# Attention B of a three-stage kernel: five batches in flight, memory summed in PSUM, norms on another engine, a new value operand, one bank of scores

## What is computed

```python
SEG, N_HEADS, dk = 64, 16, 8
def step(carry, qkv):                       # 4 segments of 64 rows, one after the other
    M, z = carry
    q, k, v = qkv
    sq = _sigma(q)                          # elu(x) + 1 = max(x, 0) + exp(min(x, 0))
    denom_q = jnp.sum(sq * z[:, :, None, :], axis=-1, keepdims=True) + EPS
    A_mem = jnp.matmul(sq, M) / denom_q
    scores = jnp.matmul(q, jnp.swapaxes(k, -2, -1)) * inv_sqrt_dk
    scores = jnp.where(causal, -jnp.inf, scores)
    A_dot = jnp.matmul(jax.nn.softmax(scores, axis=-1), v)
    A_s = beta * A_mem + (1.0 - beta) * A_dot
    sk = _sigma(k)
    denom_k = jnp.sum(sk * z[:, :, None, :], axis=-1, keepdims=True) + EPS
    V_prev = jnp.matmul(sk, M) / denom_k
    M_new = M + jnp.einsum('bhtk,bhtv->bhkv', sk, v - V_prev)
    z_new = z + jnp.sum(sk, axis=-2)
    return ((M_new, z_new), A_s)
```

## Time and profile before

| | us |
|---|---|
| median of 3 runs | 1576.78 |
| lowest and highest | 1570.99, 1587.72 |
| the profiled execution | 1586.89 |
| its span, first to last instruction | 1585.1 |
| of it, attention B | from 959.5 to the end |

### The profile page before, as it was taken

How to read it: one execution, slowest core, us unless ns; L and a number is a source line. 1 busy time by engine, 2 the same in 40 slices (tenths; PEclk the granted TensorE clock), 3 DMA queues, 4 the chain that set the end, 5 groups by cost and what they waited for, 6 DMA issues and landing times. The chain is left out here.

```text
span 1585.1 us, 52984 instructions
## 1 busy us (share of the span) xinstructions
PE 1328.7 (84%) x16996; PEld 1165.0 (73%) x16996; DVE 1095.4 (69%) x3074; ACT 873.5 (55%) x2020; POOL 927.5 (59%) x1340
## 2 busy tenths in 40 slices
PE   5999999999999999999477873787887778887786
PEld 4898998899888988999456652576666667666675
DVE  4467787788777887888344444667677777767874
ACT  2466766666666666676356652444454544444442
POOL 4456766667667666775478873445445554444551
PEclk9899999999999999999789995879799998879996
DMA  4523322332233223331144422434344444334331
GB/s 136 159 85 104 101 77 82 89 99 80 79 89 99 78 81 89 99 91 51 44 127 121 134 70 74 111 109 119 105 127 119 116 121 124 106 104 117 112 117 46
DMA packets 181701, 158.23 MB, mean 100 GB/s; under 512 B 12529, under 2 KB 163185, under 8 KB 181618
## 3 DMA queue, kind: packets, MB, share of 16 engines
q1 hardware_dynamic: 181618, 157.17, 35.1%
HBM read 113.09 MB, written 44.04 MB: 99 GB/s over the span
## 5 line engine op out<-in xcount | busy, mean ns | idle before, releaser
L609 PE MATMUL a_bank<-a_vp,a_prob 128*128 128x74 f32 x4096 | 598.0, 253 | 0.0
L609 PEld LDWEIGHTS a_bank<-a_vp,a_prob 128*128 128x128 f32 x4096 | 587.8, 192 | 5.5
L697 DVE TENSOR_REDUCE a_nmax<-a_bank 128x2 f32<-128x512 f32 x512 | 344.9, 685 | 156.9 <-PE a_bank L578 156.7
L496 ACT ACTIVATE a_prob<-a_bank 128x512 f32<-128x512 f32 x512 | 305.5, 597 | 216.0 <-PE a_bank L593 210.7
L578 PE MATMUL a_bank<-a_k_st,a_q_st 96*128 96x256 bf16 x1024 | 259.5, 276 | 38.3 <-DVE a_nmax L697 25.2
L593 PE MATMUL a_bank<-a_q_st,a_k_st 120*128 120x256 bf16 x1024 | 281.5, 275 | 2.2 <-POOL a_q_st L345 2.2
L416 POOL TENSOR_TENSOR a_prod<-a_ov,a_wgt 128x512 f32<-128x512 f32 x128 | 152.5, 1192 | 34.1 <-POOL a_prod L416 17.2
L345 POOL TENSOR_SCALAR a_q_st<-a_mt 24x2048 bf16<-24x2048 bf16 x64 | 121.5, 1898 | 82.6 <-ACT a_mt L470 36.9
L578 PEld LDWEIGHTS a_bank<-a_k_st,a_q_st 96*128 96x128 bf16 x1024 | 128.9, 134 | 50.0 <-DVE a_nmax L697 32.1
L1504 ACT ACTIVATE c_prob<-c_bank 128x256 f32<-128x256 f32 x256 | 98.8, 386 | 101.4 <-PE c_bank L1596 97.1
L593 PEld LDWEIGHTS a_bank<-a_q_st,a_k_st 120*128 120x128 bf16 x1024 | 140.1, 137 | 11.0 <-issue 2.6
(11 more groups left out here) (205 smaller groups left out, 2821.2 us busy)
## 6 DMA issues: line engine op xcount, KB each, us to landing
a_q_st<-scratch_a_parts_dram SPq DMA_DIRECT2D x64, 288.0 KB
a_k_st<-scratch_a_parts_dram SPq DMA_DIRECT2D x192, 96.0 KB
c_q_st<-scratch_c_parts_dram SPq DMA_DIRECT2D x64, 288.0 KB
c_k_st<-scratch_c_parts_dram SPq DMA_DIRECT2D x192, 96.0 KB
scratch_a_parts_dram<-a_parts SPq DMA_DIRECT2D x32, 384.0 KB, 2.7
scratch_c_parts_dram<-c_parts SPq DMA_DIRECT2D x32, 384.0 KB, 2.7
a_x<-in_x SPq DMA_DIRECT2D x32, 128.0 KB, 3.5
scratch_y<-a_y SPq DMA_DIRECT2D x32, 128.0 KB, 3.1
```

Of the source, the lines that this page charges most:

```text
L496: act.activation(prob[h % 4][:, :, :].rearrange("p a b -> p (a b)"), t_ps[h % 2][:, :], ACT.Exp).then_inc(exped, 1)
L609: mm = pe.matmul(o_ps[g % 2][:, at:at + VM], prob[h % 4][:, c, t * P:(t + 1) * P], vp[o][:, c, 0:VM], start=c == 0, stop=c == NT - 1)
L697: dve.tensor_reduce(nmax[:, t, 2 * g:2 * g + 2, 0], s_ps[t][:, :].rearrange("p (h k) -> p h k", h=2), AX.X, ALU.max, negate=True).then_inc ...
```

## The change

- Five batches are in flight in place of four. Of the memory, segment 0 stays at lag 1 (steps 6 and 7) and segments 1 and 2 move to the next iteration, lag 2 (steps 1, 2 and 4, 5). x4's chain moves to lag 4.
- The memory is summed in PSUM: update 1 and 2 add to what is in ps_c. DVE masks the sum once a segment, and the addition to mz and the tile mzt are gone. Reads go to other columns of the same bank.
- z4 is normalised on ACT and not on DVE. POOL computes the statistics of both norms in one set of four instructions at the start of its body, ahead of the split.
- max(kq, 0) is made by ACT (Relu), min(kq, 0) by POOL after the split, both by DVE before. The factor 8^-0.5 moves from q into the exponential's scale.
- The value operand vb is copied by ACT straight from PSUM in two instructions; the tile vs and POOL's four copies are gone.
- There is one bank of scores in place of two. Score units are at steps 1, 3, 5, 7. The maxima are split once a batch, 32 wide. The freed bank lets z and z4 have their own (ps_d).
- The shifted units start at step 3 of lag 2 (OFF = 3) and end at step 2 of lag 3. Before they started at step 7 of lag 1.
- SP issues half 0 of batch n at the end of its body as before, but half 1 of batch n - 1 near the start of the next body.
- The transposes of z, z4, ad and am are written as matmuls against the identity in two column halves. Those of sg and of the maxima stay transposes.
- The kq matmuls move from step 1 to step 0, and z's transpose from step 0 to step 7 of the iteration before.

```diff
-        S_AT = (1, 2, 4, 5)
-        OFF = 7
...
+        SU, ST, STAGES = 4, 8, 5
+        BROWS = SEG + NPART * H
+        READ_AT = (MW, 2 * MW, MW)
+        S_AT = (1, 3, 5, 7)
+        OFF = 3
...
-        ps_a, ps_b, ps_c, s_ps, t_ps, o_ps = *bank[0:3], bank[3:5], bank[5:7], bank[7]
-        mt_ps = ps_a[SEG:BROWS, 0:T // 2].bitcast(BF16)
+        ps_a, ps_b, ps_c, ps_d, s_ps, o_ps, t_ps = *bank[0:6], bank[6:8]
+        z_ps, w_ps = ps_d[:, 0:T], ps_b[:, 0:T]
+        O_W = NT * H * (HD + 1)
+        mt_ps = ps_b[SEG:BROWS, 0:T // 2].bitcast(BF16)
...
+                def stack(b, o, h2):
+
+                    hs = slice(h2 * H // 2, (h2 + 1) * H // 2)
+                    if later(j, b, 2):
+                        sp.wait_ge(shifted, (b - 2) * ST + (h2 + 1) * ST // 2)
+                        apart(sp, spare)
+                    sp.dma_start(q_st[o][0:SROWS, hs, :], left(parts_dram[o, NPART:2 * NPART], hs)
+                                 ).then_inc(stack_in[o][h2], 16)
+                    for a in range(NPART):
+                        sp.dma_start(k_st[o][a * NPART * HD:(a + 1) * NPART * HD, hs, :],
+                                     right(parts_dram[o, 0:NPART], hs)).then_inc(stack_in[o][h2], 16)
...
+                if active(j, u, 1):
+                    stack(n - 1, 1 - i, 1)
...
+                    sp.dma_start(xt[i][:, :, :], x_dram[at[0], at[1]]).then_inc(xt_in, 16)
...
+                    sp.dma_start(wc[1 - i][:, :, :].rearrange("p a f -> p (a f)"), wc_dram[at[0]]).then_inc(wc_in, 16)
                 if active(j, u, 0):
...
-                    stack(0)
-                    stack(1)
-                if active(j, u, 3):
-                    at = pair(j, u, 3)
-                    sp.wait_ge(x4_d, n - 2)
+                    stack(n, i, 0)
+                if active(j, u, 4):
+                    at = pair(j, u, 4)
...
+                ks = slice(0 if active(j, u, -1) else 1, 2 if active(j, u, 4) else 1)
+                if ks.start == 0:
...
+                pool.tensor_scalar(var[:, ks, :], mv[o][:, ks, :, 1], EPS, 1.0, ALU.add, ALU.mult
...
+                pool.tensor_tensor(rs[:, ks, :], var[:, ks, :], half[:, ks, :], ALU.pow).then_inc(norm_d, 1)
...
+                    if later(j, n, 1):
+                        pool.wait_ge(nexp_d, n)
+                    apart(pool, spare)
+                    pool.tensor_scalar(neg[:, :, :], kq[i][:, :, :], 0.0, 1.0, ALU.min, ALU.mult).then_inc(neg_d, 1)
+                if active(j, u, 4):
...
-                        act.activation(prob[g % 4][:, :], t_ps[g % 2][:, 0:T], ACT.Exp).then_inc(exped, 1)
-                    if s == 0 and active(j, u, 1):
+                        act.activation(prob[g % 4][:, :], t_ps[g % 2][:, 0:T], ACT.Exp, scale=HD ** -0.5
...
+                    if s == 2 and active(j, u, 2):
+                        act.wait_ge(mt_p, n - 1)
+                        act.copy(late[i][SEG:BROWS, :], mt_ps).then_inc(mt_d, 1)
...
+                        act.copy(flat(kq[i]), ps_a[:, :]).then_inc(kq_d, 1)
+                        if later(j, n, 1):
+                            act.wait_ge(sg_d, n)
+                        act.activation(flat(pos), ps_a[:, :], ACT.Relu).then_inc(pos_d, 1)
...
+                        for p in range(2):
+                            act.copy(own_values(vb[o], p)[:, :, :, 0:HD],
...
+                        for t in range(NT):
+                            act.activation(z4[:, t, :], x3[i][:, t, :], ACT.Identity, scale=rs[:, 1, t:t + 1],
...
+                        for t in range(NT):
+                            act.activation(z[o][:, t, :], x[o][:, t, :], ACT.Identity, scale=rs[:, 0, t:t + 1],
...
+                    b = n - lag
+                    if c == 0:
+                        pe.wait_ge(v_d, b * VD + 1)
+                        if later(j, b, 1):
+                            pe.wait_ge(read_d, b * READ)
+                    elif c == 1:
+                        pe.wait_ge(u_d, b * 2 + 1)
+                    else:
+                        pe.wait_ge(read_d, b * READ + 5)
+                    columns(ps_c[:, 0:MW], skn[st][:, c, :], uv[st][:, c, :], start=c == 0, skip=True
...
+                    pe.wait_ge(mz_d, b * 3 + c + 1)
+                    for a in range(2):
+                        mm = pe.matmul(ps_c[a * SEG:(a + 1) * SEG, READ_AT[c]:READ_AT[c] + MW],
+                                       sg[st][:, a, (c + 1) * SEG:(c + 2) * SEG], mz[:, :], start=c == 2, stop=True,
...
+                    if s == OFF:
+                        values(s)
...
-                        columns(t_ps[g % 2][:, 0:T], pick[:, g % (ST // 2), :, :].rearrange("p a k -> p (a k)"),
-                                late[g // (ST // 2)][:, :])
+                        columns(t_ps[g % 2][:, 0:T], pick[:, g, :, :].rearrange("p a k -> p (a k)"), late[st][:, :])
...
-                        if w >= 2 or later(j, b, 1):
-                            pe.wait_ge(maxed, b * SU + w - 1)
-                        columns(s_ps[t][:, :], ident16[:, :], causal[:, :])
+                        if w or later(j, b, 1):
+                            pe.wait_ge(maxed, b * SU + w)
+                        columns(s_ps[:, :], ident16[:, :], causal[:, :])
...
+                    if s == 0 and active(j, u, 0):
+                        pe.wait_ge(zt_d, n + 1)
+                        batches(pe, at_d, j, n - 3, 2)
+                        columns(ps_a[:, 0:T], w_kq[:, 0, :], flat(zt[i]))
+                        columns(ps_a[:, T:2 * T], w_kq[:, 1, :], flat(zt[i])).then_inc(kq_p, 1)
+                    if s == 1 and active(j, u, 1):
+                        pe.wait_ge(sg_d, n)
+                        batches(pe, x3_d, j, n - 3)
...
+                            mm = pe.transpose(ps_b[0:SEG, c * P:(c + 1) * P], sg[o][:, 0, c * SEG:(c + 1) * SEG], ident[:, :])
...
+                    if s == 1 and active(j, u, 2):
+                        update(2, 1, i)
+                    if s == 2 and active(j, u, 2):
+                        read(2, 1, i)
...
+                remember(2, 1)
+                reduce_unit(0)
+                read(2, 1, i)
+                divide(3)
+                reduce_unit(1)
+                remember(2, 2)
+                reduce_unit(2)
+                read(2, 2, i)
...
+                remember(1, 0)
...
+                    dve.tensor_tensor(flat(x4[i]), z_ps, flat(xb[i]), ALU.add).then_inc(x4_d, 1)
+                reduce_unit(3)
+                read(1, 0, o)
...
+                    dve.tensor_tensor(flat(x3[o]), w_ps, flat(xt[o]), ALU.add).then_inc(x3_d, 1)
+                split_max()
+                if active(j, u, 3):
+                    dve.wait_ge(x3_d, n - 2)
+                    moments(1, n - 3, x3[o], mv[i])
...
+                    moments(0, n + 2, x[i], mv[i])
```

More of the change, by code:

```diff
@@ L1619, in body @@
                         mm.then_inc(score, 1)
-                    if s == 0 and active(j, u, 1):
-                        b = n - 1
-                        pe.wait_ge(sg_d, b + 1)
-                        if later(j, b, 1):
-                            pe.wait_ge(read_d, b * 9)
+                    if s not in (OFF, OFF + 1):
+                        values(s)
+                    if s == 1 and active(j, u, 2):
+                        b = n - 2
+                        pe.wait_ge(mp_d, (b + 1) * MP)
+                        batches(pe, x3_d, j, n - 3)
+                        apart(pe, spare)
+                        for t in range(NT):
+                            mm = pe.transpose(mt_ps[:, t * P:(t + 1) * P],
+                                              mpart[:, t, :, :].rearrange("p a h -> p (a h)"), ident16[:, :])
+                        mm.then_inc(mt_p, 1)
@@ L1651, in body @@
-                    if s == 0 and active(j, u, 3):
+                    if s == 1 and active(j, u, 2):
+                        update(2, 1, i)
+                    if s == 2 and active(j, u, 2):
+                        read(2, 1, i)
+                    if s == 4 and active(j, u, 1):
+                        pe.wait_ge(sk_d, 2 * n)
+                        batches(pe, mt_d, j, n - 1)
+                        for c in range(NS):
+                            for a in range(2):
+                                mm = pe.matmul(ps_b[a * SEG:(a + 1) * SEG, c * P:(c + 1) * P], zt[o][:, c, :],
+                                               w_v[:, :], start=True, stop=True)
+                        mm.then_inc(v_p, 1)
@@ new lines, in body @@
+                    if s == 4 and active(j, u, 2):
+                        update(2, 2, i)
+                    if s == 5 and active(j, u, 2):
+                        read(2, 2, i)
+                    if s == 4 and active(j, u, 4):
+                        b = n - 4
+                        pe.wait_ge(z4_d, (b + 1) * NT)
+                        batches(pe, zt_d, j, n + 1)
+                        for t in range(NT):
```

(34 more changed lines are left out.)

626 lines of the change are left out of this document (249 added, 377 removed).

## The result

| | before | after |
|---|---|---|
| median of 20 runs, us | 1575.97 | 1584.59 |
| lowest and highest | 1562.63, 1587.72 | 1575.34, 1596.93 |
| the profiled execution | 1586.89 | 1583.46 |
| its span | 1585.1 | 1581.6 |

The ratio of after to before is 1.0062, with a 95% interval of 1.0040 to 1.0084. So the change made the kernel about 9 us longer, within the 1% that was called no change. The forecast was 1537 us and faster. The time lies inside the range, but on the wrong side of the kernel before.

What follows compares the result with a forecast made beforehand. A chain bounds B, PE waiting for DVE's am; afterwards two half-load legs: 1.8 + 2.1 + 2 x (0.2 + 6.1) = 16.5, plus 0.3: 16.8. Span 983.7 + 31 x 16.8 + 40.5 = 1545.0; plus 1.8, less 10.1: 1537 us, range 1481 to 1595.

Steps and rivals of the forecast that it cites:

- the likeliest case: Attention B: both halves' DMA waits outlast PE's queue and add up; a half 5.6 to 6.7 us, period 15.8 to 18.0, chance 0.48.
- a slow stretch is partly covered by the DMA leg: 0.3 us a batch: Clock falls after PE's idle stretch at step 5 were claimed to add only 0.3 us, making the period 16.8.
- only 128 to 256 KB follow directly, so I take 6.1 for each: Each half's load, from first issue to its waiting score unit, was claimed to take 6.1 us, with little traffic behind it.
- the 10.1 us taken off for the profiled execution: The median was taken as 10.1 us below the profiled execution, turning 1546.8 into 1537 us.
- The second rival: New legs eat the gain: 6.9 us a half, or moments, norms and split adding a us; period 18.1, 1577 us, chance 0.12.
- no cost: Loads of x, xt and wc, moved behind the waits for the halves and needed an iteration later, were claimed to cost nothing.
- B: The shifted unit of step 6, after which half 0's buffer is free for its next load.
- The "hidden" rival: Halves land in 5 us and stay hidden, DVE's order sets the time; period 15, 1481 us, chance 0.17.
- The forecast's own band for a half, 5.6 to 6.7: Time of one half's load in us allowed by the forecast, with period 15.8 to 18.0, 1506 to 1574 us, chance 0.48.
- 1016 + 31 x period: Formula giving the median time in us from the period of a batch, with the 10.1 us already taken off.
- 0.04 of the band's 0.48: Share of the forecast's 0.48 chance counted as the same time as before; the other 0.44 was counted as faster.

## Why the forecast of "faster" was wrong, step by step

The mechanism was the one of the likeliest case: two legs of waiting for a half, added in one ring. Its sizes were too small, and three steps of the prediction failed: the clock, "a slow stretch is partly covered by the DMA leg: 0.3 us a batch", which measured about 0.9; "only 128 to 256 KB follow directly, so I take 6.1 for each", which measured 6.64 for half 1; and the 10.1 us taken off for the profiled execution. The second rival, the new legs eating the gain, at 1577 us and a chance of 0.12, comes nearest in time, but by luck: neither its halves of 6.9 us nor the parts on the path are in the trace. The miss is 1584.6 - 1537 = 47.6 us, and it divides so:

| term | forecast | measured | us |
|---|---|---|---|
| 31 periods | 16.8 each | (1540.55 - 985.55) / 31 = 17.90 | +34.2 |
| score unit 0 of batch 0 | 983.7 | 985.55 | +1.8 |
| behind unit 0 of batch 31 | 40.5 | 1581.6 - 1540.55 = 41.05 | +0.6 |
| from the span to the median, rounded | -8.0 | +3.0 | +11.0 |

The two ends of the 31 periods, unit 0 of the first and of the last batch:

```profile
985.55 0.64 PE L1566 MATMUL c_bank<-c_causal,c_ident 128*64 128x512 bf16 x2 [4.29 <-DMA c_k_st<-scratch_c_parts_dram]
...
1540.55 0.41 PE L1566 MATMUL c_bank<-c_causal,c_ident 128*64 128x512 bf16 x2 [2.89 <-DMA c_k_st<-scratch_c_parts_dram]
```

**The period, leg by leg.** Means over 26 cycles of after:

| leg | forecast | measured |
|---|---|---|
| half 0's issue to unit 0 | 6.1 | 6.12 |
| unit 0 to half 1's issue | 1.8 + 0.2 | 2.29 |
| half 1's issue to unit 2 | 6.1 | 6.64 |
| unit 2 to half 0's issue | 2.1 + 0.2 | 3.14 |
| clock falls, spread | 0.3 | in the legs |
| sum | 16.8 | 18.19 |

(These middle cycles are a little longer than the mean over all 31.)

- *Half 1's transfer* is 0.54 too short. The step "only 128 to 256 KB follow directly, so I take 6.1 for each" took one value for two places that differ. Behind half 0 stand 256 KB: the store of x4 3.3 us after the half's first issue and the load of x 4.3 us after it, in the mean. Behind half 1 stand 640 KB: xt at 3.3 us, wc at 4.2 and the parts' write, 384 KB, at 4.9. The sum left out the parts' write, and said of moving xt and wc behind half 1 "no cost". Without these two, half 1 took 6.11.
- *The clock falls* are the other large one: 0.84 on the last leg and 0.11 on the second, where 0.3 had been set aside for the whole period. Where the clock stays up, the last leg takes 2.28, as forecast. Where it falls it takes up to 4. One such cycle, the group of unit 2 and what follows, and the granted clock (third figure from the end) of the two stretches behind the wait:

```profile
1329.81 0.41 PE L1566 MATMUL c_bank<-c_causal,c_ident 128*64 128x512 bf16 x2 [2.45 <-DMA c_k_st<-scratch_c_parts_dram]
...
1331.29 1.07 PE L1566 MATMUL c_bank<-c_ident,c_ad 128*64 128x128 f32 x8
...
1332.99 0.43 PE L1633 MATMUL c_bank<-c_q_st,c_k_st 128*64 128x64 bf16 x8
1333.53 0.81 SPq L1307 DMA_DIRECT2D c_q_st<-scratch_c_parts_dram  x1
```

```profile
1329.00:1331.00 2.00, 1.19 (x28) 1.10 (x30) 0.42 (x1) 0.32 (x1) 0.00 (x0) 0.81 0.91 259
1331.00:1333.00 2.00, 2.00 (x28) 1.96 (x27) 0.99 (x4) 0.00 (x0) 0.00 (x0) 0.50 0.00 0
```

  PE stood 2.45 us, the clock is at 0.50, the 1.2 GHz level, from 1331 to 1333, and the eight matmuls of ad take 1.07 us where they took 0.61 in the cycle at full clock above. Half 0's issue comes 3.72 us behind unit 2. The prediction said that "a slow stretch is partly covered by the DMA leg". This is the step that failed: the wait comes *before* the slow stretch, and the part of it between unit 2 and B delays the next issue, so nothing covers that part. That filling the wait brought the leg back to 2.30 and saved 14 us shows it.
- *The 0.3 itself* was misread from the trace of before. It is the mean period less 17.83, taken for a period "with the clock up"; but the granted clock of those 17.83 us is 0.90. The windows of one period whose clock did stay up, and of that one:

```profile
1275.62:1292.33 16.71, 13.56 (x306) 10.95 (x301) 13.00 (x45) 8.78 (x23) 9.00 (x16) 1.00 0.44 116
1311.94:1329.77 17.83, 14.96 (x305) 12.14 (x303) 13.11 (x45) 8.67 (x22) 9.00 (x16) 0.90 0.44 122
```

  From unit 0 to unit 0, 12 of the 31 periods of before have a clock of 1.00, and their mean is 17.3 against 18.2 for all: 0.9 a batch. In after 7 periods have 1.00, with a mean of 17.0 against 17.9 for all: 0.9 again. With 0.9 for 0.3 the forecast would have been 31 x 0.6 = 19 us longer. These are differences between periods, and a long wait can make both the fall and the length; the filled wait is the direct test.
- *The queue between* was 0.29 short where unit 0 leads to half 1's issue. At full clock it is 2.18; the other 0.11 is the clock. A buffer is free at the end of the shifted unit's last matmul, 0.41 us after its start, where 0.24 from start to start was counted; PE's queue before it takes 1.67 for 1.55; and SP issues 0.10 behind that end, where 0.2 was taken.

**The offset.** The profiled execution of before was 10.1 us above the median of its kernel, and the sum took this off for after too. After's profiled execution lies 1.1 us *below* its median. The offset was that of one execution and says nothing of the next kernel; without it the forecast would have been 1547. It makes 11 of the 48 us and none of the mechanism.

**What held.** DVE is at 216.7 / 22 = 9.9 us a batch (forecast at most 10.3). PE's waits for am are gone. Half 0's issue comes 0.1 us behind the end of B. The single bank of scores costs nothing that the waits show. The drain cost 3.5 us where 3 was taken. The "hidden" rival (period 15, 1481 us) was wrong about the halves, but near in size to what lay under them: with the buffers free in time the periods were 14.4 and 13.9. That chain was DVE's last moments, POOL's norms and split, and the parts' write.

**The chances.** The forecast's own band for a half, 5.6 to 6.7, held both measured values, and the band for its period, 15.8 to 18.0, held 17.9; it reached the edge by half 1, the clock and the queue all going one way, and the offset put the time beyond. That the time still lies inside the outer range, 1481 to 1595, says little for the sum. By the prediction's own form, 1016 + 31 x period, a period above 17.6 is no longer faster by 1%; without the offset, 1026 + 31 x period, it is one above 17.3. Only 0.04 of the band's 0.48 had been counted there, although allowed far longer halves than 6.1, and the earlier trace rows a batch with a long fall of the clock 4.8 us longer than the one before it.

## What to carry to other kernels

When a change moves the last use of a buffer back, count the other engines' queue between that release and the next need, against the time that the refill takes from its first issue: two buffers refilled in turn, each asked for too late, add up into the period, and one step of distance at each (here a list of four numbers) was worth 108 us. Write down the whole ring of waits with a length for each leg, and price the slower clock on the leg that follows a wait, not on the average; take as the period without falls only one whose granted clock is 1.00. Never carry the distance of one profiled execution from its median into the forecast of another kernel.

## What was not expected of the hardware

- The wait of 2.45 us that ends at 1329.81 was followed by the 1.2 GHz level (0.50 from 1331), though PE worked on both sides of it; the one of 2.14 us that ends at 1310.84 was not. Eight pairs of spare matmuls in the wait raised the clock of the stretch from 0.91 to 0.99. The Trainium skill, page "TensorE: Matmul & The Clock Gate", Part 1, subsection "HAM oscillation — how this bites in real kernels", describes a wait for a DMA in each tile and a slow start of the next tile behind it. This trace agrees in part: the leg behind the wait is 0.84 us longer in the mean, but in 6 of 26 batches the clock stayed up there (2.28 to 2.29 us).
- A half of 576 KB in four DMAs from one queue takes 6.1 us to its waiting matmul with 256 KB issued behind it, 6.6 with 640 KB, 4.4 with an eighth of its own bytes, and 2.9 of each is the issuing.
- On POOL a pass with two constants over 128x512 fp32 takes 0.62 us where it multiplies and adds with bf16 output, and 1.93 where it takes the minimum and multiplies with fp32 output (rows of after, start and duration). Which of the two differences it is was not tried. The split is ahead of it in POOL's queue.

```profile
1304.80 0.62 POOL L1421 TENSOR_SCALAR c_parts<-c_kq 128x512 bf16<-128x512 f32 x1
...
1309.21 1.93 POOL L1429 TENSOR_SCALAR c_neg<-c_kq 128x512 f32<-128x512 f32 x1 [0.29 <-POOL c_parts L1424]
```
